# A vision transformer in five passes: six image buffers instead of four in both attentions, another order in the embedding, and transfers of 99 rows cut into 96 and 3

## The chip, the core and the metric

The kernel runs on one core of a Trainium2 chip. The metric is the device time of one execution in microseconds. Five engines work side by side, each through its own list of instructions: TensorE (PE; its weight loads are PEld), VectorE (DVE), ScalarE (ACT), GpSimd (POOL) and SyncE (SP), which here issues every DMA. They wait for each other through semaphores only.

## The reference, cut to what matters

```python
def tok(images):                                  # 128 images, 196 patches of 768 numbers
    tokens = einsum('npi,di->npd', patches, W_map) + b_map
    tokens = concat([class_token, tokens]) + positional       # 197 rows of 192
    x = (tokens - mean) / sqrt(var + eps) * ln_w + ln_b       # over rows and columns of an image
    q, k, v = (x per head) @ Wq, Wk, Wv + biases              # 12 heads of 16
    return tokens + softmax(q @ k.T / 4) @ v
def attn(x):                                      # causal: masked entries get weight zero
    q, k, v = split(x @ W_qkv)
    return softmax(mask(q @ k.T * D**-0.5)) @ v @ W_out + b_out
h = tok(x)
h = layernorm(h + attn(h))
h = layernorm(h + ffn(h))                         # 64 slots, each its own two-layer network
```

## The kernel before

Five passes follow each other, each over all 128 images, with scratch tensors in HBM between them: `embed_pass` (to about 1024 us of the profile), `attend_pass` with `causal=False` (names `a_`, 1028 to 2765), `attend_pass` with `causal=True` (names `c_`, 2769 to 4150), the routing (`r_`), the experts (`x_`) and the combination (`o_`). An image of 198 rows (197 and one of padding) lies in two tiles of 99 partitions.

**Pipelines.** In each pass every engine runs `pipeline(eng, n, depth, R, step)`: step c works on several images at once, on image c - 1 for one job, on c - 2 for the next and so on; `b3` is image c - 3. The order of the work on an engine is the order in which `step` writes it. The first steps are written out, then a hardware loop whose body holds R steps runs over most of the images, then the last ones are written out. R is also the number of places for an image's data (`place` is the image modulo R, `parity` modulo 2). R is 4 in the embedding and in the attentions. With 128 images and a depth of 7 the loop of an attention holds 120 steps.

**Embedding.** On TensorE a step is: the sum for the mean of image c - 2 (L374, `e_statp`), the transposes of c - 3 (L380, `e_xtp`), half of the tokens of c - 1 (`token_tile(b1, 0)`, L365), the variance of c - 2 (L391), q, k (L399) and v (L404) of c - 3, and the other half of the tokens of c - 1. VectorE makes tokens with positions, and their row sums, of the finished half tiles (L351); L374 of the next step needs them. ScalarE makes the squares (L293), copies the transposes to SBUF (L297), takes the root (L300), and rounds q and k to bf16 (L173); VectorE takes what is left of them (`e_rest`, L345), GpSimd cuts that into two more bf16 parts (L275, L277). SyncE loads `e_ptT` and stores tokens and v (`e_tv`, 99 rows) and the parts (96 rows).

**Attentions.** The scores are made twice: once as queries by keys (`sq`, L788), of which VectorE takes the maximum of each row (L738), and once as keys by queries (`sk`, L810), with the maximum taken off within the same product: the negative maxima, cut into three bf16 parts (`mxp`, GpSimd, L578 to L585), are brought by three DMAs of one row each (L541) into rows of `qs` that meet rows of ones in `ks`. TensorE waits for them at the head of the step (`max_in_place`). ScalarE takes the exponentials (L679), the causal pass cuts with GpSimd (L601), TensorE sums (L825) and turns (L831), VectorE normalises (`on`, L761). In the first attention GpSimd adds the tokens (`a_res`, L650), which TensorE transposes in the next step (L877) and ScalarE copies (`a_hTh`, L682, once per image); from this q, k and v of the second attention are made (L840, L848), parted and stored. In the second the output projection follows. `c_hTl` (L743) is what VectorE leaves of the transpose.

SyncE's step in an attention is: the stores of image c - 7 (L529, or L532 and L535), the maxima's rows of c - 3 (L541), the load of tokens and v of c - 1 (L546), for which it waits until GpSimd has done `added` of image c - 5, and the six loads of q and k parts of image c (L554). GpSimd's `a_res` waits for the stores of image b5 - 2, since `res` and `parts` have two buffers.

Before a pass begins, all engines meet; then SyncE loads constants and VectorE sets zeros and ones in `vx` and `ks` and splits the weights into `wh` and `wl` (L716 to L723); TensorE and GpSimd wait for `ready`, that is, for all of it.

## Time and profile before

| | |
|---|---|
| median of 3 runs | 5207.82 us (5204.32 to 5209.99) |
| the profiled execution | 5199.24 us, its span 5197.5 us |
| TensorE, busy | 4585.4 us, 88% of the span |
| VectorE, ScalarE, GpSimd, busy | 3025.4, 2768.0, 2665.6 us |
| mean granted TensorE clock | 0.953 of full speed |
| DMA | 789.87 MB, 692799 packets |

A busy TensorE is counted by modelled ends of its matmuls. A row of waits says who stood idle, who ended the idle time, and how often; idle time of an engine on which nothing else waits costs nothing. The table by stretches shows how the limit changes from pass to pass.

### The profile page before, as it was taken

The page shows a single profiled execution, that of the slowest core. Times are in us where ns is not written, and L with a number is a line of the kernel's source. Part 1 is how long each engine was busy: PE and PEld are TensorE (multiplying, and loading weights), DVE is VectorE, ACT ScalarE, POOL GpSimd, SP SyncE. Part 2 cuts the span into 40 slices and gives each one's busy share as a digit, 9 for nine tenths or more (in the row PEclk, how much of TensorE's full clock was granted, in tenths as well). Part 3 has the DMA queues.
Part 4 walks back from the last instruction along what each step waited for, and adds up shares of the span by engine and source line. Part 5 has one row for each costly group of instructions (what it writes and reads, how often), then busy time and mean ns, then how long its engine had stood idle before and what let it go on. Part 6 is the DMA issues. An engine that isn't in the chain of part 4 may idle for free. (4 is left out here: it accounts for less than half of the span.)

```text
span 5197.5 us, 159359 instructions
## 1 busy us (share of the span) xinstructions
PE 4585.4 (88%) x48245; PEld 3916.5 (75%) x48311; DVE 3025.4 (58%) x8734; ACT 2768.0 (53%) x6788; POOL 2665.6 (51%) x4485
## 2 busy tenths in 40 slices
PE   7999999789999999999997999999999888889975
PEld 7888888767777777777775777777777666668953
DVE  3444444466666666666665666666666589980048
ACT  3334343356666666665663555555555467773446
POOL 2333333345555555555554666666666568881125
PEclk9999999989999999999998999999999889999975
DMA  6777777667777777777765666666666423329988
GB/s 156 177 178 176 177 177 178 158 131 149 149 153 152 149 150 151 150 153 152 149 142 114 135 131 132 132 130 134 133 133 133 88 83 93 93 79 257 276 238 260
DMA packets 692799, 789.87 MB, mean 152 GB/s; under 512 B 362225, under 2 KB 514767, under 8 KB 692720
## 3 DMA queue, kind: packets, MB, share of 16 engines
q1 hardware_dynamic: 692720, 788.90, 66.4%
q8 instruction: 40, 0.66, 0.1%
q14 instruction: 39, 0.32, 0.0%
HBM read 519.30 MB, written 265.72 MB: 151 GB/s over the span
## 5 line engine op out<-in xcount | busy, mean ns | idle before, releaser
L738 DVE TENSOR_REDUCE a_mx<-a_sq 99x2 f32<-99x394 f32 x1536 | 798.3, 561 | 515.5 <-PE a_sq L788 515.2
L738 DVE TENSOR_REDUCE c_mx<-c_sq 99x2 f32<-99x198 f32 (+1 forms) x1536 | 642.0, 459 | 310.2 <-PE c_sq L788 310.0
L679 ACT ACTIVATE a_ex<-a_sk 99x792 f32<-99x792 f32 (+1 forms) x768 | 638.5, 832 | 231.1 <-PE a_sk L810 185.3
L679 ACT ACTIVATE c_ex<-c_sk 99x792 f32<-99x792 f32 (+1 forms) x768 | 512.0, 667 | 243.1 <-PE c_sk L804 172.9
L601 POOL TENSOR_SCALAR_AFFINE_SELECT c_ex<-c_ex 99x396 f32<-99x396 f32 (+1 forms) x768 | 418.8, 550 | 291.5 <-ACT c_ex L679 288.1
L365 PE MATMUL e_tokp<-e_wmap,e_ptT 128*99 128x192 f32 x3072 | 543.9, 327 | 21.3 <-DVE e_cvar L323 21.3
L810 PE MATMUL a_sk<-a_qs,a_ks 99*99 99x198 bf16 (+1 forms) x3072 | 427.0, 262 | 98.4 <-DMA a_qs<-a_mxp 98.3
L365 PEld LDWEIGHTS e_tokp<-e_wmap,e_ptT 128*99 128x99 f32 x3072 | 482.7, 167 | 21.6 <-issue 21.3
L788 PE MATMUL a_sq<-a_ks,a_qs 96*99 96x198 bf16 x3072 | 453.7, 261 | 40.1 <-DVE a_wl L723 25.1
L810 PEld LDWEIGHTS a_sk<-a_qs,a_ks 99*99 99x99 bf16 (+1 forms) x3072 | 295.3, 130 | 241.3 <-issue 237.0
L275 POOL CAST e_parts<-e_rest 96x396 bf16<-96x396 f32 x256 | 131.0, 512 | 651.7 <-DVE e_rest L345 651.7
L788 PE MATMUL c_sq<-c_ks,c_qs 96*99 96x99 bf16 (+1 forms) x3072 | 417.2, 230 | 0.0
L785 PE MATMUL c_sq<-c_maskb,c_identb 99*99 99x198 bf16 x1536 | 376.3, 262 | 27.1 <-DVE c_bout L728 23.7
L788 PEld LDWEIGHTS a_sq<-a_ks,a_qs 96*99 96x99 bf16 x3072 | 305.8, 131 | 89.0 <-DVE a_mx L738 46.6
L650 POOL TENSOR_TENSOR a_res<-a_tv,a_on 99x384 f32<-99x384 f32 x128 | 127.7, 997 | 466.0 <-DMA scr_qk<-a_parts 460.3
L825 PE MATMUL a_pvp<-a_ex,a_vx 99*32 99x198 f32 (+1 forms) x6144 | 349.9, 346 | 0.5 <-issue 0.5
L788 PEld LDWEIGHTS c_sq<-c_ks,c_qs 96*99 96x99 bf16 x3072 | 324.5, 128 | 0.0
L825 PE MATMUL c_pvp<-c_ex,c_vx 99*32 99x198 f32 (+1 forms) x6144 | 276.6, 297 | 27.8 <-issue 1.0
L293 ACT ACTIVATE e_junk<-e_tv,e_st 99x192 f32<-99x192 f32 x256 | 114.4, 447 | 346.2 <-DVE e_st L331 346.2
L664 ACT COPY c_ot<-c_pvp 128x198 f32<-128x198 f32 x384 | 124.7, 325 | 298.6 <-PE c_pvp L825 298.6
L825 PEld LDWEIGHTS c_pvp<-c_ex,c_vx 99*32 99x32 f32 (+1 forms) x6144 | 162.6, 110 | 131.3 <-DVE c_on L761 77.2
L785 PEld LDWEIGHTS c_sq<-c_maskb,c_identb 99*99 99x99 bf16 x1536 | 194.3, 126 | 57.6 <-DVE c_mx L738 31.6
(196 smaller groups left out, 11614.9 us busy)
## 6 DMA issues: line engine op xcount, KB each, us to landing
e_ptT<-in_x SPq DMA_DIRECT2D x128, 594.0 KB
x_w<-in_fc SPq DMA_DIRECT2D x128, 576.0 KB, 5.9
scr_qk<-e_parts SPq DMA_DIRECT2D x128, 445.5 KB
scr_qk<-a_parts SPq DMA_DIRECT2D x128, 445.5 KB
scr_tv<-e_tv SPq DMA_DIRECT2D x128, 297.0 KB
a_tv<-scr_tv SPq DMA_DIRECT2D x128, 297.0 KB
scr_tv<-a_res SPq DMA_DIRECT2D x128, 297.0 KB
c_tv<-scr_tv SPq DMA_DIRECT2D x128, 297.0 KB
```

Of the source, the lines that this page charges most:

```text
L275: pool.tensor_copy(parts[:, b.place, i, :, place_of(i, 1)], rest[:, u, i]).then_inc(middle.sem, 1)
L293: nc.scalar.activation(junk[:, t], tv[:, b2.place, 0, t], ACT.Square, bias=st[:, b2.place, 1:2], accum_out=st[:, b2.place, 2 + t:3 + t]).t ...
L365: mm = nc.tensor.matmul(tokp[b.parity][:, t], ptT[:, b.place, k, t * TT:(t + 1) * TT], wmap[:, k], start=(k == 0), stop=(k == KC - 1))
L601: pool.affine_select(block_of, block_of, pattern=[[0, G], [1, TT]], compare_op=ALU.is_ge, fill=0.0, base=0, channel_multiplier=-1).then_in ...
L650: pool.tensor_tensor(res[:, b5.parity, 0], tv[:, b5.place, 0], on[:, b5.parity], ALU.add).then_inc(added.sem, 1)
L664: nc.scalar.copy(ot[:, b.parity, g], pv).then_inc(o_copied.sem, 1)
L679: nc.scalar.activation(to, of, ACT.Exp).then_inc(exped.sem, 1)
L738: nc.vector.reduce_max(mx[:, b2.parity, qt, h:h + 2], sq[f % 2][:, :, 0:width], AX.X).then_inc(maxed.sem, 1)
L785: nc.tensor.matmul(bank[:, :, qt * TT:(qt + 1) * TT], identb[:], maskb[:].broadcast_to([TT, 2, TT]), start=True, stop=False, skip_group_ch ...
L788: mm = nc.tensor.matmul(bank[:, j, 0:keys], qs[0:STACK, b.place, h + j, qt * TT:(qt + 1) * TT], ks[0:STACK, b.place, h + j, 0:keys], start ...
L810: mm = nc.tensor.matmul(buf[0:rows, a, j * SP:(j + 1) * SP], ks[:, b.place, h, kt * TT:kt * TT + rows], qs[:, b.place, h, :], start=True, ...
L825: mm = nc.tensor.matmul(to, vx[0:rows, b.place, kt, G * g + j, :], of, start=(kt == 0), stop=(kt == 1), skip_group_check=causal)
```

## The change

- **Attentions:** R is 6. `res` and `parts` have three buffers (`third`, the image modulo 3). SyncE's step begins with the maxima's rows; stores and loads follow. The waits of L546 and L554 are for image c - 7 and c - 6. The body of the hardware loop holds six steps.
- **Start of an attention:** GpSimd sets the zeros and ones, with semaphores of their own; TensorE waits for the ones in step 4 and for the split weights in step 6. The weights are loaded behind the loads of step 1, and VectorE splits them at the head of step 4.
- **Embedding:** both token tiles of c - 1 are in the first half of TensorE's step, and the variance stands between q and k. ScalarE copies the transposes before the squares, and takes the root between q and k. VectorE makes the tokens before what is left of q, and root, `xn` and what is left of k after it.
- **Transfers:** each of 99 rows that stores or loads tokens and v, or stores `h_pre`, is issued as one of 96 and one of 3 rows (`SHARES`).

The core of the diff:

```diff
+SHARES = (slice(0, 96), slice(96, TT))
+ONE_TWICE = float(np.array([0x3F803F80], np.uint32).view(np.float32)[0])
@@ attend_pass
-    R = 4
+    R = 6
-        res = m.sb(X + "res", [TT, 2, 2, 2, D])
+        res = m.sb(X + "res", [TT, 3, 2, 2, D])
-            parts = m.sb(X + "parts", [CH, 2, 2, 2, PARTS, SP], BF16)
+            parts = m.sb(X + "parts", [CH, 3, 2, 2, PARTS, SP], BF16)
@@ SyncE
-                    sp.wait_ge(added.sem, added.at(b - 4))
-                    sp.wait_ge(v_spread.sem, v_spread.at(b - 4))
-                    sp.dma_start(tv[:, b.place], tv_in[b.number]).then_inc(tv_in_place.of(b), 16)
+                    sp.wait_ge(added.sem, added.at(b - R))
+                    sp.wait_ge(v_spread.sem, v_spread.at(b - R))
+                    for rows in SHARES:
+                        sp.dma_start(tv[rows, b.place], tv_in[b.number, rows]).then_inc(tv_in_place.of(b), 16)
-                    sp.wait_ge(scored_k.sem, scored_k.at(c - 4))
+                    sp.wait_ge(scored_k.sem, scored_k.at(c - R))
+                if c.is_number(1):
+                    sp.dma_start(w[:], A["wout" if causal else "wqkv2"].rearrange("(c p) d -> p c d", p=CH)).then_inc(weighed, 16)
@@ GpSimd
-            pool.wait_ge(ready, n_ready)
+            pool.memset(vx[:], 0.0).then_inc(zeroed, 1)
+            pool.wait_ge(zeroed, 1)
+            pool.memset(vx[:, :, :, :, DH:DH + 1], 1.0).then_inc(vx_ones, 1)
+            pool.wait_ge(vx_ones, 1)
+            pool.memset(ks[STACK:AUG].rearrange("p r h s -> p (r h s)").bitcast(F32), ONE_TWICE).then_inc(ks_ones, 1)
-                        pool.wait_ge(stored.of(b5 - 2), stored.at(b5 - 2))
-                        pool.tensor_tensor(res[:, b5.parity, 0], tv[:, b5.place, 0], on[:, b5.parity],
+                        pool.wait_ge(stored.of(b5 - 3), stored.at(b5 - 3))
+                        pool.tensor_tensor(res[:, b5.third, 0], tv[:, b5.place, 0], on[:, b5.parity],
@@ VectorE
+                if c.is_number(4):
+                    dve.wait_ge(weighed, 16)
+                    nc.vector.tensor_copy(wh[:], w[:]).then_inc(w_high, 1)
+                    dve.wait_ge(w_high, 1)
+                    nc.vector.tensor_tensor(wl[:], w[:], wh[:].bitcast(F32), ALU.subtract).then_inc(w_low, 1)
```

The embedding's order on TensorE. Before, one step from the loop's body; `e_tokp` are token tiles, `e_statp` the mean, `e_xtp` the transposes, `e_varp` the variance:

```order
L374 MATMUL e_statp<-e_st,e_cmean 99x1
L380 MATMUL e_xtp<-e_ident,e_xn 96x99 x4
L384 ISA
L365 MATMUL e_tokp<-e_wmap,e_ptT 99x192 x6
L388 ISA
L391 MATMUL e_varp<-e_st,e_cvar 99x1 x2
L397 ISA
L399 MATMUL e_qp<-e_xT,e_wqkv 96x198 x2
L397 REGISTER_ALU
L399 MATMUL e_kp<-e_xT,e_wqkv 96x198 x2
L404 MATMUL e_vp<-e_wqkv,e_xT 99x96 x4
L365 MATMUL e_tokp<-e_wmap,e_ptT 99x192 x6
```

The same step after:

```order
L383 MATMUL e_tokp<-e_wmap,e_ptT 99x192 x6
L394 REGISTER_ALU
L396 MATMUL e_statp<-e_st,e_cmean 99x1
L402 MATMUL e_xtp<-e_ident,e_xn 96x99 x4
L383 MATMUL e_tokp<-e_wmap,e_ptT 99x192 x6
L411 ISA
L413 MATMUL e_qp<-e_xT,e_wqkv 96x198 x2
L416 ISA
L419 MATMUL e_varp<-e_st,e_cvar 99x1 x2
L411 REGISTER_ALU
L413 MATMUL e_kp<-e_xT,e_wqkv 96x198 x2
L426 MATMUL e_vp<-e_wqkv,e_xT 99x96 x4
```

The second token tile has moved from the end of the step to a place before q, and the first to the head; the variance stands between q and k.

SyncE's order in the first attention, the head of a step from the loop's body, before (`a_mxp` are the maxima's parts, `a_parts` and `a_res` what is stored):

```order
L532 ISA
L532 DMA scr_tv<-a_res 99x768
L535 ISA
L535 DMA scr_qk<-a_parts 96x12x198
L539 ISA
L541 DMA a_qs<-a_mxp 1x12x198 x3
L544 REGISTER_ALU
L546 ISA
L546 DMA a_tv<-scr_tv 99x768
```

And after:

```order
L552 DMA a_qs<-a_mxp 1x12x198 x3
L555 REGISTER_ALU
L563 ISA
L563 DMA scr_tv<-a_res 96x768
L563 ISA
L563 DMA scr_tv<-a_res 3x768
L566 ISA
L566 DMA scr_qk<-a_parts 96x12x198
L573 ISA
L573 DMA a_tv<-scr_tv 96x768
L573 ISA
L573 DMA a_tv<-scr_tv 3x768
```

The maxima's rows are ahead of the stores instead of behind them, and the transfers of 99 rows are pairs.

## Rows read from the trace of the kernel before

**Rows 1.** Table by stretches: length, busy per engine (instructions), TensorE clock, DMA share, GB/s.
```profile
100.00:1000.00 900.00, 815.47 (x5817) 773.92 (x5816) 379.15 (x931) 360.24 (x1047) 316.75 (x466) 1.00 0.75 176
1100.00:2700.00 1600.00, 1491.42 (x17393) 1241.53 (x17392) 993.05 (x2175) 968.15 (x1691) 890.00 (x1451) 0.97 0.71 150
2850.00:4090.00 1240.00, 1128.07 (x15632) 938.63 (x15631) 814.35 (x2131) 659.32 (x1303) 760.17 (x1423) 1.00 0.65 132
```
**Rows 2.** TensorE's waits, whole span: line, waited for, us in total, times, longest.
```profile
PE a_sk L810 <- DMA a_qs<-a_mxp: 98.3, 92, 2.0
PE e_statp L374 <- DVE e_tv L351: 93.1, 128, 0.8
PE c_work L886 <- DVE c_hTl L743: 85.4, 125, 1.5
```
**Rows 3.** Timeline, embedding: start, us, engine, line, tiles, [idle before <-releaser].
```profile
506.42 0.33 PE L374 MATMUL e_statp<-e_st,e_cmean 99*99 99x1 f32 x2 [0.74 <-DVE e_tv L351]
...
514.57 0.16 DVE L331 COPY e_st<-e_statp 99x1 f32<-99x1 f32 x1 [0.43 <-PE e_statp L374]
522.34 0.16 DVE L331 COPY e_st<-e_statp 99x1 f32<-99x1 f32 x1 [0.43 <-PE e_statp L374]
```
**Rows 4.** Table by stretches, the end of one step of the embedding.
```profile
504.93:506.42 1.49, 0.75 (x5) 0.44 (x4) 0.57 (x2) 0.00 (x0) 1.41 (x3) 1.00 0.63 209
```
**Rows 5.** Waits in 1100 to 2700, of SyncE's queue and of GpSimd.
```profile
SPq L546 <- POOL a_res L650: 524.4, 121, 5.8
...
POOL a_res L650 <- DMA scr_qk<-a_parts: 457.8, 120, 5.1
```
**Rows 6.** Timeline, SyncE's queue in one step of the first attention.
```profile
1904.23 0.34 SPq L546 DMA_DIRECT2D a_tv<-scr_tv  x1
...
1909.82 3.04 SPq L541 DMA_DIRECT2D a_qs<-a_mxp  x3
```
**Rows 7.** First attention: table by stretches, timeline of a wait and of ScalarE's copy.
```profile
2022.00:2046.00 24.00, 23.80 (x291) 20.04 (x292) 16.52 (x37) 15.97 (x29) 15.07 (x25) 1.00 0.71 154
...
2009.00:2021.00 12.00, 10.41 (x92) 8.53 (x91) 5.26 (x12) 5.30 (x10) 6.23 (x11) 0.72 0.72 159
...
2010.97 0.55 PE L810 MATMUL a_sk<-a_qs,a_ks 99*99 99x198 bf16 x4 [1.59 <-DMA a_qs<-a_mxp]
...
2012.60 0.48 ACT L682 CAST a_hTh<-a_work 96x396 fp32r<-96x396 f32 x1
2027.24 0.49 ACT L682 CAST a_hTh<-a_work 96x396 fp32r<-96x396 f32 x1
2039.17 0.49 ACT L682 CAST a_hTh<-a_work 96x396 fp32r<-96x396 f32 x1
```
**Rows 8.** Timeline, second attention, the same copy.
```profile
2912.46 0.47 ACT L682 CAST c_hTh<-c_work 96x396 fp32r<-96x396 f32 x1
2923.26 0.47 ACT L682 CAST c_hTh<-c_work 96x396 fp32r<-96x396 f32 x1
2933.59 0.48 ACT L682 CAST c_hTh<-c_work 96x396 fp32r<-96x396 f32 x1
```
**Rows 9.** Timeline, the start of the first attention on VectorE and TensorE.
```profile
1033.52 7.98 DVE L719 MEMSET a_ks<- 3x9504 bf16 x1 [2.04 <-issue]
...
1043.78 0.87 PE L788 MATMUL a_sq<-a_ks,a_qs 96*99 96x198 bf16 x4 [25.15 <-DVE a_wl L723]
```
**Rows 10.** DMA queues (packets, MB, share of 16 engines) in 1110:1160, 2770:2850; 1200:2690 has q1 alone.
```profile
q8 instruction: 5, 0.08, 0.9%
...
q8 instruction: 6, 0.10, 0.6%
...
q1 hardware_dynamic: 217654, 223.94, 71.2%
```
**Rows 11.** DMA issues: count, KB each, median us from issue to landing.
```profile
scr_mix<-r_cT SPq DMA_DIRECT2D x128, 49.5 KB, 1.9
scr_mix<-x_o SPq DMA_DIRECT2D x64, 96.0 KB, 6.3
```

More of the change, by code:

```diff
@@ L76, in parity, with third, is_number @@
         return self.place % 2
+    @property
+    def third(self):
+        return self.place % 3
     def inside(self, n):
         return not isinstance(self.turn, int) or 0 <= self.number < n
+    def is_number(self, i):
+        return isinstance(self.turn, int) and self.number == i
 class Event:
@@ L289, in step @@
                 b2, b3 = c - 2, c - 3
+                if b3.inside(n):
+                    act.wait_ge(x_turned.sem, x_turned.at(b3))
+                    nc.scalar.copy(xT[0:CH, b3.parity], xtp[:]).then_inc(x_copied.sem, 1)
                 if b2.inside(n):
@@ L324, in _, with left_of @@
             dve.wait_ge(ready, READY1)
+            def left_of(b3, i, p):
+                dve.wait_ge(high.sem, high.at(b3, i + 1))
+                dve.wait_ge(low.sem, low.at(b3 - 2, i + 1))
+                nc.vector.scalar_tensor_tensor(out=rest[:, b3.parity, i], in0=p[:], scalar=SCALES[i],
+                                               in1=parts[:, b3.place, i, :, place_of(i, 0)], op0=ALU.mult,
+                                               op1=ALU.subtract).then_inc(left.sem, 1)
             def step(c):
@@ L334, in step @@
                                                    op0=ALU.add, op1=ALU.mult).then_inc(centred.sem, 1)
+                if b1.inside(n):
+                    dve.wait_ge(embedded.sem, embedded.at(b1))
+                    dve.wait_ge(stored.of(b1 - 4), stored.at(b1 - 4))
+                    nc.vector.scalar_tensor_tensor(out=tv[:, b1.place, 0], in0=tokp[b1.parity][:], scalar=1.0, in1=posb[:],
+                                                   op0=ALU.mult, op1=ALU.add,
+                                                   accum_out=st[:, b1.place, 0:1]).then_inc(tokens.sem, 1)
+                if b3.inside(n):
+                    left_of(b3, 0, qp)
+                if b2.inside(n):
                     dve.wait_ge(std.sem, std.at(b2))
@@ L400, in step @@
                         mm.then_inc(done.sem, 1)
+                    if i == 0 and b2.inside(n):
+                        pe.wait_ge(squares.sem, squares.at(b2))
+                        pe.wait_ge(std.sem, std.at(b2 - 1))
+                        for t in range(2):
+                            mm = nc.tensor.matmul(varp[:, 0:1], cvar[:, t], st[:, b2.place, 2 + t:3 + t],
+                                                  start=(t == 0), stop=(t == 1))
+                        mm.then_inc(var_p.sem, 1)
+                if b3.inside(n):
                     pe.wait_ge(v_copied.sem, v_copied.at(b3 - 1))
@@ L640, in step @@
                     if b6.inside(n):
[L641 removed]
+                        mid, low = (parts[:, b6.third, 0, :, place_of(0, a)] for a in (1, 2))
                         pool.wait_ge(q_rest.sem, q_rest.at(b6))
```

145 lines of the change are left out of this document (68 added, 77 removed).

## The prediction

> **What bounds the kernel now.** I read the table of stretches first [rows 1]: TensorE is busy 91% in the embedding, 93% in the first attention and 91% in the second; no other engine passes 66% there, and the DMA share stays at 0.75 or less. So each of these stages lasts as long as TensorE's work plus its gaps, and the list of TensorE's waits says what the gaps are [rows 2]: 98.3 us for the maxima's rows (92 times), 93.1 us in the embedding before L374 (128 times), 85.4 us for `c_hTl` in the second attention, and the two waits of about 25 us in which the attentions begin. The routing, expert and combining passes are not touched by the change, and I leave their time as it is.
>
> **Embedding: the token tiles move.** Before, an image's second token tile is TensorE's last work of a step and L374, which needs the tokens that VectorE makes of it, is the first work of the next; TensorE stands idle 0.74 us [rows 3]. After, the second tile lies in the middle of the step, and q, variance, k, v and the next image's first tile (4 to 5 us of matmuls in these rows) lie between it and L374. The wait goes: 93.1 us, of which the first and last steps may keep a little, so **-91 us**. What is late next? q now needs ScalarE's copy of `xtp` with the second tile (2.1 us) as cover, and the copy takes some 0.5 us; the variance has that tile and q as cover (2.8 us) for ScalarE's two squares of about 0.6 us each behind the copy. The Sqrt, the reciprocal and `xn` take some 1.1 us in a row and have k, v and a tile ahead of them. VectorE's second `rest` comes later, so GpSimd's parts and SyncE's stores and the load behind them do too. That load is used two steps later; by my count about 10 us are left. The other bound: the work of the DMA engines per image is 0.75 x 16 x 7.77 = 93 engine-us, 5.8 us on each; even the 11 engines that the split relieves stay below the new step of 7.04 us, but at 7.3 us a step only -60 us would be left. Bounds -60 and -93.
>
> **First attention: the maxima's rows.** In SyncE's order the loads of step c stand behind a wait for GpSimd's `a_res` (524.4 us) [rows 5]. GpSimd itself waits 457.8 us for the store of two images before [rows 5]. So loads, stores and maxima are issued in one train: seven loads from 1904.2, then two stores, and from 1909.8 the maxima's three rows, behind all of it [rows 6]. With six places and three result buffers both waits are satisfied long before, and the maxima's rows are the first thing of the step; stores and loads follow them and have until the next step's maxima, about 9 us, to drain. The data of one image are 0.71 x 16 x 13.22 = 150 engine-us, 9.4 us on each engine, so they are just gone when the next rows come; those then have some 3 us until TensorE wants them. The extra small transfers cost SyncE about 0.35 us each [rows 6], 14 issues and under 9 us in a step of 12.
>
> What the step becomes, the trace shows. Between 2022 and 2046 TensorE waits for nothing and its clock is 1.00; ScalarE's `a_hTh`, once per image, starts at 2027.24 and 2039.17 [rows 7], and with no wait the next steps take the same: 11.94 us a step. The mean is 1600 us over 121 steps [rows 5], 13.22. The difference of 1.28 is more than the 0.80 of the waits because the clock falls to its lower level after the longer ones: after a wait of 1.59 us the stretch 2009 to 2021 has clock 0.72 (the wait ends at 2010.97), and the step from 2012.60 to 2027.24 takes 14.64 [rows 7], 2.7 too long. With 0.08 for the turns of the loop (0.47 in six, next part) the step is 12.02: (13.22 - 12.02) x 122 = **-146 us**. Bounds: -98, if only the waits go, and -156.
>
> **Second attention and the starts.** There no TensorE wait is for a transfer, and its largest, for `c_hTl`, has its chain (TensorE, ScalarE, VectorE) unchanged. Its steps are 10.33 us long and each fourth 10.80 [rows 8]: the turn back of the loop costs 0.47 us. The 120 steps in the loop make 30 laps of four and 29 turns back before, 20 laps of six and 19 turns after: 10 x 0.47 = **-5 us**. At the start of an attention TensorE waits behind VectorE's memsets, the longest 7.98 us, and its split of the weights, some 2 us, until 1043.78 [rows 9], while SyncE issued the last load that it needs 12 us before, the sixth of a train that begins at 1029.2. The memsets go to GpSimd, the weights to VectorE in step 4, ahead of its maxima: about 8 us less and 2 more, so **-12 us** for the two attentions; GpSimd's memsets have no row in the trace, and if they are half again as slow as VectorE's they finish when the first maxima need GpSimd. Bounds +5 and -18. The split of 99 rows into 96 and 3 has nothing else to give: TensorE waits for none of these transfers. While one of 99 rows runs alone the DMA share is 0.63 [rows 4], some 10 or 11 of 16 engines.
>
> So far: -91 - 146 - 5 - 12 = **-254 us**.
>
> **What the change adds: a longer loop.** The attention's loop holds one step per place, so its body grows from four steps to six. The row of TensorE's instruction queue (q8) shows packets of 16.5 KB: 5 in 1110 to 1160, the first lap of the first attention's loop, and none from 1200 to 2690, although the loop turns 29 more times [rows 10]. So 5 packets of code (one per 0.8 of a step) stay in place and turning back is cheap. After, the body has 7.5 packets' worth in the first attention and, by its 108 matmuls a step against 120, a tenth less in the second, and touches 8 or 9 of them, plus the one fetched ahead. That this much stays in place the trace doesn't show. If it does not, the head of the loop is fetched anew at each of 2 x 19 turns, and TensorE stands meanwhile. The trace has no such jump. From below the price is nothing. From above: a packet of 16.5 KB occupies an engine for 0.006 x 16 x 80 / 6 = 1.3 us [rows 10]; from issue to landing a store of 49.5 KB takes 1.9 us and one of 96 KB in full traffic 6.3 us [rows 11]. I take 1.3 + 1.9 = 3.2 us, nearest to a small transfer, and since such a gap is longer than the 1.59 us after which the clock fell, the 2.7 us of that step for half of the turns: 4.55 x 38 = **+173 us**; the upper bound is 6.3 + 2.7 = 9.0 per turn, 342 us.
>
> I take it that the fetches come, since the body grows to over 1.5 times what is shown to stay. A page of the Trainium skill, "Runtime: NRT & Kernel Launch", section "Instruction fetch mechanics", speaks against this change: it gives TensorE's instruction memory 128 KiB, refilled in blocks of 16 KiB, and says that a taken branch to a block outside it stalls on a fetch. By that rule eight blocks stay, and both loops would be too long by one or two. The trace agrees on the block [rows 10]; no row shows the 128 KiB. The page also calls the window two pages, and there the trace differs: five blocks stay.
>
> Sum on the profiled execution (5199.24 us in its result, span 5197.5): 5199 - 254 + 173 = 5118. The median of the runs is 8.6 us above the profiled execution, so I forecast **5127 us**.
>
> **Rivals.** (1) *The long loops stay in place.* For it: not one fetch in 29 turns. Against: nothing of this length was run. Time 5199 - 254 + 9 = 4954 us. (2) *Slower.* The same fetch, dearer: the loops are refetched, the head's packet queues behind data and the clock falls at each turn, 9.0 us x 38 = 342, giving 5199 - 254 + 342 + 9 = 5296 us. It decides from 254 / 38 = 6.7 us per turn on. For it: the next packet, 0.2 of a packet further, may be missing as well and follow serially. Against: the five fetches of a first lap cost nothing visible. (3) *A new wait for the old.* The maxima's rows still meet the loads of the step before, which have only some 9 us to drain; half of the 146 us is not gained: 5127 + 73 = 5200 us. Against it: steps without any wait exist already, with the same bytes. That the change does not do what it says I exclude from the order of the instructions.
>
> **How the numbers follow.** Forecast 0.55, rival 1 0.22, rival 2 0.13, rival 3 0.10. The forecast's own range, by prices from 2 to 7 us per turn, is 5030 to 5220 us. The range down to rival 1 and up to this is 4940 to 5240 and leaves out rival 2 and a little more. A measurement of this kernel tells about 0.2% (10 us) from no change. Faster by more than that: forecast and rival 1 and a part of rival 3, 0.80; within it 0.05, rival 3 in the main; slower 0.15.
>
> **What the profile would show.** No wait at L374's successor; steps of the embedding near 7.04 us. No wait of `a_sk` for `a_mxp`, and clock 1.00 within a lap. `a_hTh` every 11.94 us except at each sixth step; there the gap is the price of a turn. Packets on q8 through the whole of both attentions: some 20 x 8 in each; if there are still 40 in all, rival 1 holds. Wrong would be: TensorE's gaps in the embedding filled by a wait for `e_ptT` or `e_xT`, or steps of the attention bound by VectorE.

## The result, and the profile after

The changed kernel takes 5330.1 us (median of 4 runs, 5324.2 to 5339.1), the kernel before 5208.9 in the runs beside it: a ratio of 1.022, with a 95% interval of 1.0175 to 1.0265. It is slower by 2.2%, and the interval lies clear of no change; 5127 us, 1.6% less than before, was forecast. All ratios here leave out a run that took over 1.5% longer than the fastest of its kernel, at a lower clock; there was one, 5176 us in the version with whole rows. The profiled execution took 5325.97 us (span 5324.3), against 5199.24 (5197.5) before.

TensorE's waits in the changed kernel (columns as in [rows 2]: line, waited for, us in total, times, longest):

```profile
PE a_sk L845 <- issue: 102.5, 19, 6.2
PE c_sk L845 <- issue: 79.2, 21, 4.7
...
PE c_work L927 <- DVE c_hTl L777: 75.9, 125, 1.5
...
PE c_work L918 <- issue: 47.8, 19, 3.2
PE a_work L918 <- issue: 46.4, 19, 3.5
```

The two waits that the change was to remove are gone from the top of the list: no `e_statp`, and of the 98.3 us for `a_mxp` [rows 2] one wait of 1.9 us is left. Only `c_hTl` is left of those rows, 75.9 us in place of 85.4. In their place stand four rows by "issue", which is time in which TensorE waits for nothing that the profile shows, 276 us together. The count of 19 is the number of turns back of a loop of six steps; the row with 21 holds two short ones besides, 1.8 us together, that stand outside the loop's turns. The table of DMA queues says what TensorE lacked (packets, MB, share of 16 engines; before: 40 packets, 0.66 MB in the whole span, 5 and 6 of them in the stretches of [rows 10]):

```profile
q8 instruction: 406, 6.65, 0.6%
```

Code is fetched ten times as often. One turn on TensorE in the first attention (timeline; the brackets hold the idle time and what ended it):

```profile
1046.30 0.88 PE L860 MATMUL a_pvp<-a_ex,a_vx 99*32 99x198 f32 x16
...
1048.75 0.34 PE L883 MATMUL a_pvp<-a_wh,a_hTl 96*99 96x192 f32 x2
1054.76 0.89 PE L845 MATMUL a_sk<-a_qs,a_ks 99*99 99x198 bf16 x4 [5.67 <-issue]
1055.45 0.87 PE L823 MATMUL a_sq<-a_ks,a_qs 96*99 96x198 bf16 x4
1056.11 0.37 PE L918 MATMUL a_work<-a_ident,a_res 99*96 99x99 f32 x1
1059.98 0.73 PE L918 MATMUL a_work<-a_ident,a_res 99*96 99x99 f32 x3 [3.51 <-issue]
1060.64 1.55 PE L860 MATMUL a_pvp<-a_ex,a_vx 99*32 99x198 f32 x16
```

And the table of stretches around it (columns as in [rows 1]: us, five engines, TensorE's clock, DMA share, GB/s):

```profile
1044.00:1046.00 2.00, 1.90 (x21) 1.68 (x20) 1.97 (x6) 1.28 (x2) 1.60 (x3) 1.00 0.13 31
1050.00:1052.00 2.00, 0.00 (x0) 0.00 (x0) 0.00 (x0) 0.00 (x0) 0.78 (x2) 1.00 0.88 192
1052.00:1054.00 2.00, 0.00 (x0) 0.00 (x0) 0.00 (x0) 0.00 (x0) 0.00 (x0) 0.75 0.95 170
1054.00:1060.00 6.00, 1.74 (x10) 1.41 (x10) 1.04 (x2) 0.83 (x1) 0.00 (x0) 0.50 0.44 86
1060.00:1066.00 6.00, 6.00 (x42) 4.79 (x43) 2.52 (x6) 2.54 (x5) 1.00 (x3) 0.50 0.01 3
1066.00:1068.00 2.00, 2.00 (x28) 1.67 (x27) 0.71 (x2) 0.72 (x2) 0.75 (x2) 0.84 0.00 0
```

There are two gaps in a row, 5.67 us at the branch back and 3.51 us a little further on, with a few matmuls between them. TensorE does nothing from 1049.1 to 1054.8; its clock falls to the lower level (0.50, 1.2 GHz) in 1052:1054 and comes back in 1066:1068. So the work behind the gaps runs at half speed at first: L860's 16 matmuls take 1.55 us at 1060.64, 0.88 at 1046.30.

In the second attention the lower level holds longer. At the turn of 2976 the stretches 2976:2982 and 2982:2990 have clock 0.50, and so has the next one, though TensorE is busy all through it:

```profile
2990.00:2994.00 4.00, 4.00 (x34) 3.19 (x33) 2.09 (x4) 1.16 (x2) 2.05 (x3) 0.50 0.68 189
```

ScalarE's copy `a_hTh`, once per image, shows the price of a turn in the first attention:

```profile
1038.27 0.49 ACT L718 CAST a_hTh<-a_work 96x396 fp32r<-96x396 f32 x1
1060.75 0.48 ACT L718 CAST a_hTh<-a_work 96x396 fp32r<-96x396 f32 x1 [4.13 <-PE a_work L918]
1075.38 0.49 ACT L718 CAST a_hTh<-a_work 96x396 fp32r<-96x396 f32 x1
1087.32 0.49 ACT L718 CAST a_hTh<-a_work 96x396 fp32r<-96x396 f32 x1
```

The steps are 22.48, 14.63 and then 11.94 us: the quiet step is as long as [rows 7] gave it, and this turn adds 10.5 and 2.7 us (11.4 in the mean of all, below). Over the whole trace the ledger, taken between the first and last of these copies, is:

| | before | after | difference |
|---|---|---|---|
| to the first `a_hTh` (embedding, start) | 1085.9 | 954.6 | -131 |
| first to last `a_hTh`, 127 steps | 1666.2 | 1724.0 | +58 |
| to the first `c_hTh` | 66.4 | 62.6 | -4 |
| first to last `c_hTh`, 127 steps | 1326.3 | 1539.9 | +214 |
| rest | 1052.7 | 1043.2 | -10 |

In the steps of the first attention -158 us of gain and 216 us of turns are hidden under the +58; how they come apart is seen from the run with four places below. The row "rest" is the passes behind the attentions, which the change doesn't touch; it takes 1052.7 us here and 1083.9 in another execution of the kernel before (below), so its -10 is scatter.

### The profile page after: what moved, and what is told of

Same layout as the page of the kernel before. It is cut to its first block and busy times, and to the rows that moved or that the text cites. A ratio compares the mean times of both kernels' runs of the same rounds, so it can differ in the third digit from the quotient of the medians.

```text
span 5324.3 us, 160684 instructions
## 1 busy us (share of the span) xinstructions
PE 4662.9 (88%) x48311; PEld 4013.0 (75%) x48311; DVE 3060.9 (57%) x8728; ACT 2746.4 (52%) x6788; POOL 2740.8 (51%) x4491
## 5 line engine op out<-in xcount | busy, mean ns | idle before, releaser
L845 PE MATMUL a_sk<-a_qs,a_ks 99*99 99x198 bf16 (+1 forms) x3072 | 428.8, 263 | 104.4 <-issue 102.5
L823 PE MATMUL a_sq<-a_ks,a_qs 96*99 96x198 bf16 x3072 | 457.9, 263 | 31.9 <-DMA a_ks<-scr_qk 17.2
L823 PE MATMUL c_sq<-c_ks,c_qs 96*99 96x99 bf16 (+1 forms) x3072 | 444.4, 241 | 0.0
L286 POOL CAST e_parts<-e_rest 96x396 bf16<-96x396 f32 x256 | 176.7, 690 | 482.4 <-DVE e_rest L342 482.4
L820 PE MATMUL c_sq<-c_maskb,c_identb 99*99 99x198 bf16 x1536 | 398.6, 275 | 22.7 <-DVE c_bout L757 19.3
L823 PEld LDWEIGHTS a_sq<-a_ks,a_qs 96*99 96x99 bf16 x3072 | 309.3, 132 | 80.7 <-DVE a_mx L772 46.4
L860 PE MATMUL a_pvp<-a_ex,a_vx 99*32 99x198 f32 (+1 forms) x6144 | 352.7, 349 | 0.5 <-issue 0.5
L823 PEld LDWEIGHTS c_sq<-c_ks,c_qs 96*99 96x99 bf16 x3072 | 351.5, 137 | 0.0
L860 PE MATMUL c_pvp<-c_ex,c_vx 99*32 99x198 f32 (+1 forms) x6144 | 290.5, 309 | 24.9 <-DVE c_on L795 1.3
L845 PE MATMUL c_sk<-c_qs,c_ks 99*99 99x198 bf16 x1536 | 227.4, 273 | 84.2 <-issue 79.2
L614 POOL CAST a_mxp<-a_mxn 12x198 bf16<-12x198 f32 x128 | 43.8, 342 | 478.7 <-ACT a_mxn L723 478.7
L860 PEld LDWEIGHTS c_pvp<-c_ex,c_vx 99*32 99x32 f32 (+1 forms) x6144 | 168.3, 114 | 137.0 <-DVE c_on L795 68.8
L845 PEld LDWEIGHTS c_sk<-c_qs,c_ks 99*99 99x99 bf16 x1536 | 142.9, 134 | 147.8 <-issue 108.2
```

What stands on the lines that cost most here:

```text
L286: pool.tensor_copy(parts[:, b.place, i, :, place_of(i, 1)], rest[:, u, i]).then_inc(middle.sem, 1)
L614: pool.tensor_copy(high, of).then_inc(max_high.sem, 1)
L820: nc.tensor.matmul(bank[:, :, qt * TT:(qt + 1) * TT], identb[:], maskb[:].broadcast_to([TT, 2, TT]), start=True, stop=False, skip_group_ch ...
L823: mm = nc.tensor.matmul(bank[:, j, 0:keys], qs[0:STACK, b.place, h + j, qt * TT:(qt + 1) * TT], ks[0:STACK, b.place, h + j, 0:keys], start ...
L845: mm = nc.tensor.matmul(buf[0:rows, a, j * SP:(j + 1) * SP], ks[:, b.place, h, kt * TT:kt * TT + rows], qs[:, b.place, h, :], start=True, ...
L860: mm = nc.tensor.matmul(to, vx[0:rows, b.place, kt, G * g + j, :], of, start=(kt == 0), stop=(kt == 1), skip_group_check=causal)
```

## Experiments

The runs below were made on three more chips, four kernels on each. Before takes 5149.6, 5148.5 and 5153.6 us on them, 1.1% less than on the first one, so each kernel is judged by its ratio to before on the same chip. The changed kernel takes 5320 us on the one of them on which it was run again.

**Four places instead of six.** Everything else of the change stays; result buffers are four.

```diff
-    R = 6
+    R = 4
-        res = m.sb(X + "res", [TT, 3, 2, 2, D])
+        res = m.sb(X + "res", [TT, 4, 2, 2, D])
-            parts = m.sb(X + "parts", [CH, 3, 2, 2, PARTS, SP], BF16)
+            parts = m.sb(X + "parts", [CH, 4, 2, 2, PARTS, SP], BF16)
```

> The changed kernel with four places again in both attentions, so that TensorE's loops hold four steps; all else of the change stays (maxima first, embedding's order, 96 and 3 rows; the result buffers are four). Theory (long loops are fetched anew at each turn): no gap by 'issue' at the turn, q8 packets about 42, and most of the 440 us that the turns cost is gone; embedding 6.77 us a step. If four places suffice for the loads, 4930 to 4970 us. Rival (six places themselves, or the shared DMA engines, cost the time): near the changed kernel, 5330. If the sixth and fifth place were what removed the wait for the maxima, a_sk waits for the maxima again in part of the steps: 5050 to 5130.

Measured: 4909.9 us, ratio 0.9541 (0.9525 to 0.9557), 4.6% less than before. TensorE's list of waits now begins with (`o_` is the last pass)

```profile
PE c_work L927 <- DVE c_hTl L777: 85.4, 125, 1.5
PE o_zp L1554 <- POOL o_yb L1484: 80.5, 55, 9.8
```

the queue of code holds

```profile
q8 instruction: 40, 0.66, 0.1%
```

and the stretches of both attentions read

```profile
1100.00:2400.00 1300.00, 1289.09 (x15681) 1083.64 (x15680) 891.55 (x1959) 863.17 (x1525) 810.32 (x1306) 1.00 0.76 167
2900.00:3700.00 800.00, 728.06 (x10088) 605.91 (x10091) 524.82 (x1375) 424.64 (x840) 490.80 (x919) 1.00 0.60 132
```

The same two stretches of the changed kernel:

```profile
1100.00:2400.00 1300.00, 1167.28 (x13514) 974.00 (x13515) 771.42 (x1690) 746.85 (x1314) 698.22 (x1126) 0.93 0.71 146
2900.00:3700.00 800.00, 675.81 (x8503) 562.36 (x8504) 446.99 (x1158) 359.82 (x710) 413.30 (x772) 0.88 0.53 113
```

No gap by "issue" at a turn, one wait for `a_mxp` of 2.0 us, clock 1.00. The 127 steps of the first attention take 1508.4 us (11.88 each), those of the second 1321.4. Against the changed kernel's 1724.0 and 1539.9 the 19 turns of each loop cost 216 and 218 us, 11.4 and 11.5 us each. The gain does not need six places, and this version beats both kernels.

**The long loop alone.** The kernel before, with its four places, but TensorE's attention loops hold eight steps.

```diff
-        with eng.Fori(0, (n - head) // R) as j:
+        with eng.Fori(0, (n - head) // R, m) as j:
-            for c in range(head, head + R):
+            for c in range(head, head + m * R):
...
-            pipeline(pe, n, DEPTH, R, step)
+            pipeline(pe, n, DEPTH, R, step, 2)
```

> The kernel before, with nothing changed but the body of TensorE's loop in the attentions: eight steps instead of four (15 laps instead of 30, two attentions, 14 turns each). Theory: at each turn two gaps by 'issue' of together about 8 us and a fallen clock, 11 to 12 us a turn less the 0.5 us of the turns saved: 5209 + 28 x 11.5 - 30 x 0.5 = about 5515 us, q8 packets over 300. Rival (a turn costs by what the other engines do in the changed kernel, not by the length): 5195 to 5210 us.

Measured: 5390.2 us (5366.8 and 5413.7), ratio 1.0471 (1.0415 to 1.0527). TensorE's waits:

```profile
PE c_sk L810 <- issue: 70.4, 14, 6.3
...
PE a_sk L810 <- DMA a_qs<-a_mxp: 55.8, 51, 3.0
PE a_sk L810 <- issue: 36.2, 12, 3.4
PE a_work L877 <- issue: 33.1, 14, 3.9
```

and its queue of code:

```profile
q8 instruction: 372, 6.09, 0.5%
```

The length of TensorE's code alone, with no buffer, order or transfer changed, brings the gaps: 241 us for 28 turns, 8.6 each. That is less than the 11.5 I had carried over, for two reasons. In the first attention part of each gap takes the place of a wait for `a_mxp` (85.0 us in this kernel without the long loop, 55.8 here). In the second there is no second gap: the list has a row by "issue" for `c_sk` and none for the work behind it. By the count of blocks below, the head of this loop lies at 27.3 (22.3, and 5 by which the first loop grew), early in its block, while the first one's lies at 7.77; so the block behind the head is needed much later, and one miss is left.

**The loop's head at the start of a block.** The changed kernel, but the first instruction of each of TensorE's two attention loops is placed at a block's start (`ONE` names the one engine).

```diff
-        with eng.Fori(0, (n - head) // R) as j:
+        with eng.bass.Fori(0, (n - head) // R, engines=ONE(eng), **kw) as j:
...
-            pipeline(pe, n, DEPTH, R, step)
+            pipeline(pe, n, DEPTH, R, step, head_slot={mybir.EngineType.PE: 0})
```

> The changed kernel, with the head of both TensorE loops placed on the first instruction of a fetch block; before, the heads lie 0.77 and 0.80 into one. The body of the first attention is 7.49 blocks long, that of the second 6.93. Theory that the memory holds 8 blocks, one of which is the block fetched ahead: the second attention's loop (7 blocks and one ahead) fits and its turns cost 0.5 instead of 12 us, the first's (8 and one ahead) doesn't fit, but with the head at a block's start only one gap a turn is left: about 5330 - 19 x 11.5 - 19 x 3 to 5 = 5020 to 5055 us; q8 about 42 plus 19 x 8 or 9. If 9 or more blocks are held, both fit: about 4900. If fewer, none does, and only the second gap goes: 5180 to 5250.

Measured: 5062.6 us (5060.9 and 5064.3), ratio 0.9835 (0.9815 to 0.9854). One kind of gap is left in TensorE's waits:

```profile
PE a_sk L850 <- issue: 97.4, 19, 6.3
```

and the queue of code:

```profile
q8 instruction: 216, 3.54, 0.3%
```

The second attention has no gap at a turn any more (and q8 shows no packet during its laps), the first has lost its second one. Against the version with four places a turn of the first still costs (1670.1 - 1508.4) / 19 = 8.5 us, for a gap of 5.1.

**The branch back announced.** The changed kernel, with a hint on the same two loops, issued at the head of each lap, that names the branch back.

```diff
-            pipeline(pe, n, DEPTH, R, step)
+            pipeline(pe, n, DEPTH, R, step, hint_back_edge=True)
```

> The changed kernel, with TensorE told at the head of each lap of the attentions' loops where the lap's last branch will go. Theory (the cost of the turn is the fetch of the head's block, started only at the branch): if the fetch is started ahead, the first gap of 5.4 us goes, the second of 2.4 us (the next block, 0.2 further) stays or shrinks, and the clock stays up in most turns: 5330 - 38 x 8 = 5030 us; without both 4910. Rival (the sequencer's restart itself costs the time): unchanged, 5330.

Measured: 5038.2 us, ratio 0.9778 (0.9755 to 0.9801). Here the first gap is gone and the second stays, in the first attention (6.2 us a turn for a gap of 3.7); in the second neither is left. TensorE's waits:

```profile
PE a_work L923 <- issue: 69.6, 19, 4.4
```

and the queue of code:

```profile
q8 instruction: 217, 3.56, 0.3%
```

**Both.**

```diff
-            pipeline(pe, n, DEPTH, R, step)
+            pipeline(pe, n, DEPTH, R, step, head_slot={mybir.EngineType.PE: 0}, hint_back_edge=True)
```

> The changed kernel with TensorE's attention loops of six steps, their heads at the start of a block of code and the branch back announced ahead. Theory: a turn has two misses in a row when nothing is done, the head's block and the one behind it; the head at a block's start took the second away (one gap of 5.1 us left), the announced branch took the first away (the second left, 3.7 us). Both together leave none in the first attention, its step is 11.94 and the whole as with four places, a ratio of 0.954 to 0.956. Rival: the loop's code is still larger than what stays, so one of the two gaps comes back at another place, ratio 0.975 to 0.985 as with either alone.

Measured: 4914.5 us, ratio 0.9535 (0.9496 to 0.9573). A step of the first attention takes 11.94 us, and 12.1 at the turns, as with four places. The queue of code:

```profile
q8 instruction: 45, 0.74, 0.1%
```

The first attention's stretch:

```profile
1100.00:2400.00 1300.00, 1289.04 (x15681) 1083.54 (x15682) 892.73 (x1961) 861.89 (x1525) 810.77 (x1307) 1.00 0.76 167
```

I had expected the two edits to hide two fetches. The 45 packets say more: nothing is fetched again at all. The counts of the kernels give the rule. The built list of TensorE's instructions is counted in blocks of 256 instructions, a packet of 16.5 KB each, and the last column is what q8 shows:

| kernel, loop | from block to block | touched | refetched each lap, by count of q8 |
|---|---|---|---|
| before, first | 7.77 to 12.77 | 6 | none |
| before, second | 22.3 to 26.9 | 5 | none |
| changed, first | 7.77 to 15.26 | 9 | all 9 and one more |
| changed, second | 24.80 to 31.73 | 8 | all 8 and one more |
| head at a block, first | 7.49 blocks | 8 | all 8 and one more |
| head at a block, second | 6.93 blocks | 7 | none |
| announced, first | 7.77 to 15.26 | 9 | all 9 |
| announced, second | 24.80 to 31.73 | 8 | none |
| both, first | 7.49 blocks | 8 | none |

Worked out from this table, with 45 packets for the rest, the changed kernel should fetch 19 x (10 + 9) + 45 = 406 packets (measured 406), the one with its heads at a block 19 x 9 + 45 = 216 (216), the announced one 19 x 9 + 45 = 216 (217), and the long loop alone, whose loops touch 11 and 10 blocks, 14 x (12 + 11) + 45 = 367 (372). Lap by lap the traces have the same: 10 packets on q8 in 1143:1226 of the changed kernel, a lap of its first attention, and 9 in 2906:2981, a lap of its second. So eight blocks stay. What follows is my reading of how. One is fetched ahead; at a loop's end that is the block behind the loop, a ninth in the changed kernel's second attention, and it pushes out the oldest, which is the loop's own head. From then on each block pushes out the one needed next, and every block is fetched anew in every lap; only the one at the branch, and with a late head the one right behind it, have no time to come in ahead, which fits the one gap of the long loop with its head at 27.3. An announced branch makes the head's block the one fetched ahead, so no ninth is needed. The counts fit this in all nine rows, but no row shows which block was fetched when. One more thing fits it: with the branch announced, the second attention's loop is left with a miss, a gap of 6.8 us with the hint alone (one step of 20.1 us in place of 10.4) and of 4.1 us with both, and the versions without the hint have no gap there.

The Trainium skill, "Runtime: NRT & Kernel Launch", section "Instruction fetch mechanics", gives TensorE 128 KiB in blocks of 16 KiB. The trace agrees: eight blocks. Its window of two pages is not what these runs show; a loop that fits the eight blocks turns back without any fetch.

**Before again.** The kernel before, unchanged, for its trace on one of these chips.

> The kernel before, unchanged, for its trace on the chip of these comparisons, where its runs were at 5150 us against 5208 on the first chip. Theory: the difference lies in the first attention's wait for the maxima's rows, since that hangs on transfers; its step there is then about 12.75 us instead of 13.22, and embedding (7.75 us a step) and second attention (10.45) are as before. Rival: the difference is spread over all stages, 1.1% in each, as it would be if the chip were simply a little faster.

Measured: 5186.0 us in this one execution, the first attention's 127 steps 1618.9 us, on the first chip 1666.2. Embedding and second attention are alike within 4 us. TensorE's wait for the maxima's rows:

```profile
PE a_sk L810 <- DMA a_qs<-a_mxp: 85.0, 109, 1.7
```

The first attention's stretch:

```profile
1100.00:2400.00 1300.00, 1221.41 (x14579) 1014.00 (x14578) 829.99 (x1822) 809.38 (x1417) 742.10 (x1216) 1.00 0.73 155
```

The chips differ where TensorE waits for transfers, in the first attention: within its loop 12.85 us a step here, 13.23 there. The wait itself is 85.0 us in place of 98.3; most of the rest of the 47 us goes with the clock, 1.00 here and 0.97 there. The stages behind the attentions took 1083.9 us in this execution, 1052.7 on the first chip, so its total is closer to that chip's than its rounds' median of 5148 is.

**The changed kernel again.**

> The changed kernel as it is, on the chip of the other comparisons, where before takes 5148 us. Theory: what the chips differ in is the first attention's wait for the maxima's rows (12.86 us a step here, 13.25 on the first chip, all other steps alike); the changed kernel has no such wait, so its time stays near 5325, a ratio of about 1.034 here. Rival: the chip is 1.1% faster in everything, then 5270 us and a ratio of 1.022 as on the first chip.

Measured: 5319.8 us, ratio 1.0333 (1.0286 to 1.038). The changed kernel has the same time on both chips, the kernel before has not: without the wait for the maxima's rows it does not matter how fast a chip brings them. Its steps of the first attention take 1720.6 us here and 1724.0 there. The 1.1% by which the change looks worse here is the old kernel's wait, with the clock that fell behind it.

**The embedding alone.** The kernel before with the changed kernel's embedding pass.

```diff
                 b = c - 4
                 if b.inside(n):
                     sp.wait_ge(v_copied.sem, v_copied.at(b))
-                    sp.dma_start(scr["tv1"][b.number], tv[:, b.place]).then_inc(stored.of(b), 16)
+                    for rows in SHARES:
+                        sp.dma_start(scr["tv1"][b.number, rows], tv[rows, b.place]).then_inc(stored.of(b), 16)
...
+                if b1.inside(n):
+                    pe.wait_ge(loaded.of(b1), loaded.at(b1))
+                    pe.wait_ge(tokens.sem, tokens.at(b1 - 2))
+                    token_tile(b1, 0)
```

> Only the embedding is as in the changed kernel (its order and its transfers of 96 and 3 rows); the attentions are those of before. Theory from the trace after: a step of 6.77 instead of 7.75 us, 0.98 x 127 = 125 us less, a ratio of 0.976. Rival, the sum on record: 91 us less, a ratio of 0.982, and what the changed kernel's embedding gained beyond that came from elsewhere (its neighbours' transfers). Neither expects a change in the attentions' steps.

Measured: 5029.2 us, ratio 0.9771 (0.9755 to 0.9788), 119 us less; to the first `a_hTh` the traces have 961.4 instead of 1084.7, 123 less. The steps of the attentions are unchanged (12.85 and 10.47). So it is the embedding itself that gives more than the 93.1 us that its row in the list of waits holds. The groups by line in 300 to 800 us show where it is, in the weight loads (busy us, mean ns, idle us before them and what ended it), first of the kernel before:

```profile
L374 PEld LDWEIGHTS e_statp<-e_st,e_cmean 99*99 99x99 f32 x128 | 15.9, 164 | 67.0 <-DVE e_tv L351 50.1 <-issue 16.9
```

then of the changed one:

```profile
L396 PEld LDWEIGHTS e_statp<-e_st,e_cmean 99*99 99x99 f32 x148 | 24.4, 167 | 0.0
```

500 us hold 64.5 steps of 7.75. The weight loads stand idle 67.0 / 64.5 = 1.04 us a step before L374, while the matmuls show only 0.73: of these 1.04 us 0.78 (50.1 us) are put down to the wait for `e_tv` and the rest to "issue". The step fell by 0.98, from 7.75 to 6.77, and the weight loads of L396 have no idle time left. So a wait costs TensorE more than the idle time of its matmuls; that it is the start of the pipeline of loads and matmuls behind each wait is argued, not shown.

**Which part took away the wait for the maxima.** Three runs change only the order in SyncE's step, the number of result buffers, or both, each against the version with four places. First the maxima behind the stores, with four buffers:

```diff
-                b = c - 3
-                if b.inside(n):
-                    sp.wait_ge(max_low.sem, max_low.at(b))
-                    for a in range(PARTS):
-                        sp.dma_start(qs[STACK + a:STACK + a + 1, b.place], mxp[:, b.parity, a]).then_inc(max_in_place.of(b), 16)
                 b = c - 7
...
+                b = c - 3
+                if b.inside(n):
+                    sp.wait_ge(max_low.sem, max_low.at(b))
+                    for a in range(PARTS):
+                        sp.dma_start(qs[STACK + a:STACK + a + 1, b.place], mxp[:, b.parity, a]).then_inc(max_in_place.of(b), 16)
```

> As the version with four places, but SyncE issues the maxima's three rows behind the stores of the step, in the place that they have before; four result buffers stay. Theory 1 (the result buffers are what counts, since they free the stores): no wait for a_mxp, the first attention's step 11.94 us, the ratio to before as with four places, 0.954. Theory 2 (the place in the queue counts): the rows stand behind some 145 KB of stores and wait for them, 0.5 to 1 us a step and the lower clock with it, a ratio from 0.965 to 0.98.

Measured: 4912.5 us, ratio 0.9534 (0.9518 to 0.9551), no wait for `a_mxp`, steps of 11.94. The buffers suffice; the place in the queue gives nothing.

Then the same with two buffers, by the parity of the image:

```diff
-        res = m.sb(X + "res", [TT, 4, 2, 2, D])
+        res = m.sb(X + "res", [TT, 2, 2, 2, D])
...
-                        pool.wait_ge(stored.of(b5 - 4), stored.at(b5 - 4))
+                        pool.wait_ge(stored.of(b5 - 2), stored.at(b5 - 2))
```

> As the version with four places, but with the two result buffers of before and the maxima's rows behind the stores: the attentions' buffers and SyncE's order are those of before, the embedding, the starts and the split transfers those of the changed kernel. Both theories (buffers, place in the queue) expect the wait for a_mxp back; in this chip's terms 5150 - 125 (embedding) - 12 (starts) = 5013 us, a ratio of 0.973. If it stays at 0.954, neither was the cause, and the split of the 99 rows or the starts are what took the wait away.

Measured: 5015.3 us, ratio 0.9737 (0.972 to 0.9753), as expected. The wait and the stretch:

```profile
PE a_sk L845 <- DMA a_qs<-a_mxp: 74.5, 101, 1.5
```

```profile
1100.00:2400.00 1300.00, 1223.37 (x14591) 1015.22 (x14590) 830.45 (x1822) 810.30 (x1418) 741.18 (x1213) 1.00 0.71 155
```

Against the embedding alone (0.9771) it is 14 us faster, with about 8 us of scatter in either: that is what the new starts of the attentions are worth. Of these, to the first `a_hTh` the trace shows 7. And the two buffers cost 5015 - 4913 = 103 us by the medians and 1620.0 - 1508.4 = 112 by the 127 steps, for 74.5 us of waits. The clock is 1.00 over the stretch, but not in every step: behind a few of the longest waits it fell (0.80 in 1644.16:1658.71, a step of 14.55 us).

Last the maxima first, as in the change, but with two buffers:

> As the version with four places, but with the two result buffers of before; the maxima's rows stay first in SyncE's step. The run with two buffers and the maxima behind the stores had the wait (74.5 us, a ratio of 0.974), the run with four buffers and the maxima behind the stores had not (0.953). Theory 1: only the buffers matter; GpSimd still waits for the stores, so everything of a step is issued late, the wait stays near 75 us and the ratio at 0.974. Theory 2: each of the two edits is enough by itself; maxima issued first pass the loads and stores, the wait goes and the ratio is 0.954.

Measured: 5397.1 us, ratio 1.045 (1.0398 to 1.0503), by the ratios (1.045 - 0.9737) x 5150 = 367 us slower than with the maxima behind the stores. Neither theory had this. The steps of the first attention take 1978.2 us in place of 1620.0, those of the second 1359.7 in place of 1321.5. Waits of TensorE, GpSimd and SyncE's queue:

```profile
PE a_work L918 <- POOL a_res L686: 123.2, 61, 3.3
PE a_work L918 <- issue: 123.1, 64, 3.7
```

```profile
POOL a_res L686 <- DMA scr_qk<-a_parts: 686.4, 124, 6.8
```

```profile
SPq L573 <- POOL a_res L686: 636.8, 124, 5.6
```

and one step on GpSimd, then on SyncE's queue:

```profile
2044.26 0.99 POOL L686 TENSOR_TENSOR a_res<-a_tv,a_on 99x384 f32<-99x384 f32 x1 [6.83 <-DMA scr_qk<-a_parts]
```

```profile
2035.51 2.41 SPq L552 DMA_DIRECT2D a_qs<-a_mxp  x3
2038.18 0.84 SPq L563 DMA_DIRECT2D scr_tv<-a_res  x2
2039.26 0.34 SPq L566 DMA_DIRECT2D scr_qk<-a_parts  x1
2045.41 0.79 SPq L573 DMA_DIRECT2D a_tv<-scr_tv  x2
```

SyncE's queue is in order, so what is put first brings its wait with it: the maxima's rows wait for GpSimd's maxima of this step, and the stores behind them are issued only at 2038.2. With two buffers GpSimd's next `a_res` waits for the landing of just these stores (until 2044.26), and TensorE's L918 waits for `a_res`. Half of L918's waits are put down to "issue", but q8 has 40 packets here as before, so no code is missing; they have the same place and size as those put down to `a_res`. The step takes 15.7 us, 3.8 more than the quiet one. The waits are 2.0 of it (246.3 us over 125 steps); the larger part of what is left goes with the clock, which is at 0.88 over this attention:

```profile
1100.00:2700.00 1600.00, 1392.10 (x14634) 1154.26 (x14635) 845.43 (x1830) 826.18 (x1423) 750.45 (x1224) 0.88 0.55 127
```

With four buffers the stores have two steps more and the order is harmless, and so it is with three in the changed kernel, where no such wait shows.

**The rows of 99 as one transfer.** The version with four places, without the split.

```diff
-SHARES = (slice(0, 96), slice(96, TT))
+SHARES = (slice(0, TT),)
```

> As the version with four places, but each transfer of 99 rows goes as one, as before. Theory (on record: TensorE waits for none of these transfers): the ratio stays at 0.954, and what moves is the DMA share, higher by a few hundredths or not at all. Rival: the embedding's transfers of 99 rows on 10 or 11 of 16 queues make its new step of 6.77 us longer, to about 7.0 us (the share of 0.76 was already near what one of 99 rows alone reaches), 30 us more, a ratio of 0.960; or the maxima's rows find the queues busier and the wait for a_mxp comes back in part.

Measured: 4913.6 us, ratio 0.9533 (0.948 to 0.9586). The steps are 6.77, 11.93 and 10.48 us. The split changes nothing in the time; the DMA share of 1100:2400 is 0.78 without it and 0.76 with it.

## Where the prediction was right and wrong

- **The longer loop, the step that failed.** That the loops do not stay in place was forecast, and the price of a turn was to decide. I put it at 4.55 us, at most 9.0; it is 11.4 and 11.5. The sum for 38 turns is 434 us instead of 173. Two things were missing. First, there are two fetches in series per turn, not one: the head lies at 0.77 and 0.80 of a block, so the block behind it is needed a few matmuls later. I named this in rival 2 ("may be missing as well and follow serially") and gave it no price in either bound. The mean gaps are 102.5 / 19 = 5.4 and 46.4 / 19 = 2.4 us in the first attention, (79.2 - 1.8) / 19 = 4.1 and 47.8 / 19 = 2.5 in the second. Second, I had taken a fallen clock for half of the turns only; the stretches' clock of 0.93 and 0.88 and the turn shown say that it falls at the turns in general, and it stays down behind the gap: what is left of the price over the gaps, 11.4 - 7.8 = 3.6 us and 11.5 - 6.6 = 4.9 us, is, by the turns shown, mostly matmuls at the lower level, which holds longer in the second attention, where I had 2.7 from a gap of 1.59 us. The single fetch was also longer than my 3.2 us: 5.1 us where it alone is left in the first attention (head at a block), 3.7 where the second alone is.
- **Rival 2** is what happened: the mechanism, the side of the deciding point (6.7 us per turn) and that two fetches follow each other. Its 5296 us fell 34 short. By its sum it was near, but in part by luck: it had one gap of 6.3 us and 2.7 for the clock, where there are two gaps and more for the clock. Its chance of 0.13 was too low. The price of an event that the trace doesn't show had its ends from a small store and from one in traffic, and I took it near the small one; with a deciding point of 6.7 inside my bounds of 0 to 9.0, the chance should have been spread over them.
- **That the loops would not stay** was right, but for a weaker reason than there was. The second attention, 6.93 blocks long, would have stayed at another place in the blocks.
- **Embedding**: the wait is gone as forecast and no new one came. The term was -91 (at most -93); measured alone it is -119 to -123, in the changed kernel's steps 0.98 x 127 = -125. The failing assumption is that the listed wait is all that a gap costs.
- **First attention without the turns**: step 11.94 and clock 1.00 as forecast; 1508.4 - 1666.2 = -158 against -146 and a bound of -156. In [rows 7] I put the excess over the waits down to the clock. With two buffers on another chip, where the clock was 1.00 but for a few steps, 74.5 us of waits still cost 103 to 112. In the steps with 0.7 to 1.0 us of wait the excess is 0.2 us on average, so a part of it is the cost of the gap itself, as in the embedding, and not the clock.
- **What removed the wait**: I gave it to six places, three buffers and the new order together. It is the buffers (four, with four places, suffice by themselves; three with four places were not run). The new order is worth nothing with enough of them and costs 367 us with two.
- **Second attention's turns** -5: with its head at a block's start the loop of six steps is not refetched and takes 10.444 us a step, the loop of four 10.475; over 120 steps that is 4 us, about as forecast. **Starts** -12: right. The two waits in which the attentions begin are 17.2 and 19.3 us in the changed kernel, 25.1 and 23.7 before, 12 us less. **Split of rows** 0: right.
- **Sum of the gains**: -254 forecast. By the ledger it is 126.8 - 434 = -307, of which -10 is the scatter of the passes behind. The prediction's time was wrong by 203 us, 261 from the turns less 53 from the gains and a few from the medians; that the gains were larger than forecast hid a fifth of the error of the turns.

## What to carry to other kernels

Before a loop's body is made longer, count its code in blocks: by the counts above it turns back without a fetch on TensorE while the blocks that it touches and the one fetched ahead are eight or fewer, and beyond that every lap fetches everything; here a lap then paid some 11 us at the branch with two gaps, 6 to 9 with one. Aligning the head saved a block, and announcing the branch the one fetched ahead. If a buffer count sets the unroll (one step per place), give the buffers that a wait needs, and not the loop. In an in-order DMA queue the most urgent transfer put first puts its own wait first as well, so ask what behind it is waited for; and a short gap on TensorE costs more than its row of idle time; in the embedding the weight loads' idle time was nearer to it (1.04 us, 0.98 gained).

## What the runs showed of the hardware

- By the counts of packets TensorE keeps eight blocks of 16.5 KB of code, by my reading one of them fetched ahead. Going one over makes 9 to 10 fetches per lap, not one (406 packets against 45).
- A missed block stopped TensorE for 2.4 to 5.4 us in the mean, by the place of the miss; in the turn shown the DMA share was 0.88 to 0.95 during the longer stop. Whether traffic lengthens it stays open: the first gap is 5.4 us in the first attention of the changed kernel and 4.1 in the second, which has a lower DMA share (0.71 and 0.53), but with the long loop alone it is 3.0 and 5.0, the other way, and no run changed the traffic alone.
- After gaps of 5.7 and 3.5 us the clock was at 0.50 in 1060:1066, all of which TensorE was busy, and at 0.84 in 1066:1068.
- The time of the kernel before depends on the chip by 1.1%, that of the changed kernel by 0.2%; the difference sits in the stage with a wait for transfers, in the wait and in the clock behind it.
- Announcing the branch and placing the head cost little: 4914.5 us against 4909.9 and 4912.5 for the versions with loops of four steps. The trace shows one price of the announcement, the miss behind the second attention's loop: its 127 steps take 1334.0 us, 1318.3 with the head placed alone.
